# Graph attention layer 1: sums of destination groups alternate between two PSUM places and are copied straight to rows in four pieces

## The reference

```python
def gat_layer(x, W, a_src, a_dst, bias, src, dst, heads, out_c, concat):
    n = x.shape[0]
    h = (x @ W).reshape(n, heads, out_c)
    ...
    ex = jnp.exp(e - m[dst])
    z = jax.ops.segment_sum(ex, dst, num_segments=n)
    alpha = ex / (z[dst] + 1e-16)
    msg = h[src] * alpha[:, :, None]
    out = jax.ops.segment_sum(msg, dst, num_segments=n)
    ...
    return out + bias
...
x = x + _L0_gnn_ref(_layernorm(x, axis=-1), edge_index, ...)
x = x + _L0_ffn_ref(_layernorm(x, axis=-1)[None], ...)[0]
```

## Time and profile before

| | us |
|---|---|
| time, median of 3 runs | 2793.61 |
| lowest and highest of them | 2791.96 to 2797.63 |
| the profiled execution's own time | 2813.5 |
| its span, first to last instruction | 2811.7 |

### The profile page before, as it was taken

One profiled execution on the slowest core, in us unless ns is written; L12 is line 12 of the kernel. 1 busy time (PEld: TensorE's weight loads), 2 busy tenths in 40 slices (PEclk: granted clock), 3 DMA queues, 4 the chain that ended last, 5 costly groups with the idle time before them and its releaser, 6 DMA issues. The chain is left out here.

```text
span 2811.7 us, 45815 instructions
## 1 busy us (share of the span) xinstructions
PE 1794.2 (64%) x14517; PEld 1177.2 (42%) x14518; DVE 1248.1 (44%) x2621; ACT 806.2 (29%) x2172; POOL 1264.5 (45%) x1248
## 2 busy tenths in 40 slices
PE   2747668755555556555678935555555568899970
PEld 1324445433333333333344513333333356677750
DVE  7625658465656556566475051111111126221216
ACT  2400001323333333343122413333333332233320
POOL 4065561076767667710411256666666600112116
PEclk9968889956667566778899966676666777899995
DMA  5313221287877778851797988989898972445549
GB/s 184 97 41 74 68 48 35 95 256 248 253 247 250 254 250 254 261 190 45 189 251 195 259 251 303 316 308 309 306 314 312 315 259 103 129 163 163 165 175 403
DMA packets 185256, 586.03 MB, mean 208 GB/s; under 512 B 40189, under 2 KB 56572, under 8 KB 184930
## 3 DMA queue, kind: packets, MB, share of 16 engines
q0 software_dynamic: 87216, 374.99, 43.4%
q1 hardware_dynamic: 72626, 140.92, 14.9%
q10 hardware_dynamic: 25344, 69.32, 6.4%
HBM read 482.25 MB, written 96.45 MB: 206 GB/s over the span
## 5 line engine op out<-in xcount | busy, mean ns | idle before, releaser
L1437 PE MATMUL acc<-ring,work 128*32 128x192 f32 x1952 | 183.6, 489 | 149.1 <-ACT work L1495 73.3
L1373 POOL DMA_INDIRECT ring<-feat_tab,islot x196 | 231.7, 1182 | 95.7 <-issue 45.7
L1631 PE MATMUL acc<-ring,work 128*32 128x192 f32 (+1 forms) x1952 | 172.7, 494 | 124.6 <-issue 90.7
L862 PE MATMUL acc<-wg,work 128*128 128x384 f32 x600 | 232.1, 532 | 24.2 <-issue 17.4
L1553 POOL DMA_INDIRECT ring<-feat_tab,src_t x196 | 195.3, 996 | 111.9 <-issue 51.8
L1179 PE MATMUL acc<-wg,work 128*128 128x384 f32 x600 | 215.6, 509 | 24.0 <-ACT work L1236 21.5
L812 POOL DMA_INDIRECT edges<-score_tab,src_p x168 | 165.0, 982 | 127.7 <-PE tps L850 56.2
L1410 DVE TENSOR_TENSOR ring<-ring,edges 128x768 f32<-128x768 f32 x196 | 183.0, 956 | 81.7 <-DMA ring<-feat_tab,islot 72.5
L1441 PEld LDWEIGHTS acc<-edges,work 128*32 128x32 f32 x982 | 151.2, 155 | 110.8 <-issue 11.8
L1631 PEld LDWEIGHTS acc<-ring,work 128*32 128x32 f32 x1952 | 90.9, 148 | 184.6 <-issue 168.5
L1631 PE MATMUL acc<-work 128*32 128x192 f32 x1104 | 98.4, 470 | 98.1 <-issue 68.9
(11 more groups left out here) (378 smaller groups left out, 3743.5 us busy)
## 6 DMA issues: line engine op xcount, KB each, us to landing
slot_out<-ring SPq DMA_DIRECT2D x57, 384.0 KB
feat_tab<-work ACTq DMA_DIRECT2D x50, 384.0 KB
ring<-lo_rows SPq DMA_DIRECT2D x49, 256.0 KB
edges<-in_w_slow SPq DMA_DIRECT2D x28, 384.0 KB, 9.9
edges<-in_w_hebb POOLq DMA_DIRECT2D x28, 384.0 KB, 7.7
edges<-in_w_fast POOLq DMA_DIRECT2D x28, 384.0 KB, 9.4
unit_sum<-edges SPq DMA_DIRECT2D x28, 384.0 KB, 6.7
agg_raw<-work ACTq DMA_DIRECT2D x25, 388.0 KB
```

Source lines behind the costliest of these rows:

```text
L862: m = nc.tensor.matmul(acc[:, sl * 2 + c, 0:C // 2], xT[sl][:, k, :], wg[:, k, c * (C // 2):(c + 1) * (C // 2)], start=(k == 0), stop=(k = ...
L1373: pool.indirect_dma_start(rows[k][:, 0:C], None, feat_tab[l], bass.IndirectOffsetOnAxis(ap=islot[:, h * UN + k:h * UN + k + 1], axis=0)).t ...
L1437: m = nc.tensor.matmul(sums_ps[c * WIN:(c + 1) * WIN, 0:CHUNK], hot, row[:, c * CHUNK:(c + 1) * CHUNK], start=start, stop=True, skip_group ...
L1631: m = nc.tensor.matmul(sums_ps[c * WIN:(c + 1) * WIN, 0:n], hot, row[:, c * CHUNK:c * CHUNK + n], start=start, stop=True, skip_group_check ...
```

## The change

The sums of group q now go to PSUM place q % 2 (`acc[:, 0]` or `acc[:, 1]`) and no longer all to `acc[:, 0]`. ACT copies them from there straight to the rows, in four pieces (three of 32 x 192 and one of 32 x 200), with no stage between, and raises `flushed` after the fourth; `flushed` begins at one, so that opening group b waits for the flush of group b-2 instead of b-1. There are two opening matrices, and each is made one group sooner (groups 1 and 2 ahead of the loop, q + 3 after the flush of q), in place of q + 2. The small matmul of `close` writes to another PSUM tensor (`tps`). DVE waits for `flushed` instead of `blk_ready`. The wait for `raw_used`, which was ahead of the copies from stage, is now ahead of the copies out of PSUM. Since the place is part of a matmul's address, PE keeps its number in a register and has each `sums` twice in the code, behind a branch on it.

```diff
@@
-            sums_ps = acc[:, 0, 0:CHUNK + ZC]
-            zp = 3 * WIN
+            next_x = [onehot_x, stage[0][:, 0:WIN]]
@@
-                        dve.wait_ge(blk_ready, (b + 1) * WPB)
+                        dve.wait_ge(flushed, (b + 1) * WPB + 1)
@@
-                            m = nc.tensor.matmul(sums_ps[c * WIN:(c + 1) * WIN, 0:n], hot, row[:, c * CHUNK:c * CHUNK + n],
+                            m = nc.tensor.matmul(acc[c * WIN:(c + 1) * WIN, bank, 0:n], hot, row[:, c * CHUNK:c * CHUNK + n],
@@
-                        nc.tensor.matmul(acc[0:WIN, 1, 0:1], iota_f[:, 0:WIN], iota_f[:, 0:1], start=True, stop=True,
+                        nc.tensor.matmul(tps[0:WIN, 0, 0:1], iota_f[:, 0:WIN], iota_f[:, 0:1], start=True, stop=True,
@@
+                    bank_reg = pe.alloc_register("bank1")
+                    pe.reg_mov(bank_reg, 0)
+
+                    def added(i, k, bank):
+                        if k % BATCH == 0:
+                            pe.wait_ge(hot_in[k // BATCH], i * 16 + 16)
+                        pe.wait_ge(row_in[k], i * 16 + 16)
+                        sums(onehot[:, k, :], k, bank, False).then_inc(tile_mm, 1)
+
+                    def opened(b, k, bank):
+                        pe.wait_ge(open_ready, b)
+                        pe.wait_ge(flushed, b)
+                        sums(next_x[bank], k, bank, True).then_inc(open_mm, 1)
@@
-                            if k % BATCH == 0:
-                                pe.wait_ge(hot_in[k // BATCH], i * 16 + 16)
-                            pe.wait_ge(row_in[k], i * 16 + 16)
-                            sums(onehot[:, k, :], k, t, False).then_inc(tile_mm, 1)
+                            bank = pe.snap(bank_reg, min_val=0, max_val=1)
+                            with pe.If(bank > 0):
+                                added(i, k, 1)
+                            with pe.Else():
+                                added(i, k, 0)
@@
                                 with pe.Fori(b0 + 1, b1 + 1) as b:
-                                    pe.wait_ge(open_ready, b)
-                                    pe.wait_ge(flushed, b)
-                                    sums(onehot_x, k, t, True).then_inc(open_mm, 1)
+                                    pe.reg_mov(bank_reg, b & 1)
+                                    bank = pe.snap(bank_reg, min_val=0, max_val=1)
+                                    with pe.If(bank > 0):
+                                        opened(b, k, 1)
+                                    with pe.Else():
+                                        opened(b, k, 0)
@@
                         if q < NW:
-                            act.wait_ge(open_mm, q)
-                            nc.scalar.activation(onehot_x, hot_open[:, q * WIN:(q + 1) * WIN], ACT.Copy).then_inc(open_ready, 1)
+                            if q >= 3:
+                                act.wait_ge(open_mm, q - 1)
+                            nc.scalar.activation(next_x[q % 2], hot_open[:, q * WIN:(q + 1) * WIN], ACT.Copy).then_inc(open_ready, 1)
@@
+                    act.sem_inc(flushed, 1)
                     act.wait_ge(table_ready, 1)
                     next_hot(1)
+                    next_hot(2)
@@
                             act.wait_ge(closed, q + 1)
-                            nc.scalar.activation(stage[w % 2], sums_ps, ACT.Copy).then_inc(flushed, 1)
-                            next_hot(q + 2)
                             if w == 0 and b >= 2:
                                 act.wait_ge(raw_used, b - 1)
-                            act.wait_ge(flushed, q + 1)
                             for c in range(4):
-                                nc.scalar.activation(raw[b % 2][w * WIN:(w + 1) * WIN, c * CHUNK:(c + 1) * CHUNK],
-                                                     stage[w % 2][c * WIN:(c + 1) * WIN, 0:CHUNK], ACT.Copy)
-                            nc.scalar.activation(raw[b % 2][w * WIN:(w + 1) * WIN, C:ROW],
-                                                 stage[w % 2][zp:zp + WIN, CHUNK:CHUNK + ZC], ACT.Copy).then_inc(blk_ready, 1)
+                                n = CHUNK + ZC if c == 3 else CHUNK
+                                ins = nc.scalar.activation(raw[b % 2][w * WIN:(w + 1) * WIN, c * CHUNK:c * CHUNK + n],
+                                                           acc[c * WIN:(c + 1) * WIN, q % 2, 0:n], ACT.Copy)
+                            ins.then_inc(flushed, 1)
+                            next_hot(q + 3)
```

More of the change, by code:

```diff
@@ L1521, in aggregate_rows @@
                 sem(n + L) for n in ("hot_made", "open_hot", "tile_mm", "open_mm", "ones", "open_table"))
-            closed, flushed, blk_ready, zero_set, batch_mm, raw_used = (
-                sem(n + L) for n in ("closed", "flushed", "blk_ready", "zero_set", "batch_mm", "raw_used"))
+            closed, flushed, zero_set, batch_mm, raw_used = (
+                sem(n + L) for n in ("closed", "flushed", "zero_set", "batch_mm", "raw_used"))
             chain_v, bias_in, sq_in, sq_out, sum_ready, norm_ready = (
@@ L1625, in _, with sums @@
                 def _(pe):
-                    def sums(hot, k, t, start):
+                    def sums(hot, k, bank, start):
                         row = rows[k]
@@ L1642, in _ @@
                     for c in range(4):
-                        m = nc.tensor.matmul(sums_ps[c * WIN:(c + 1) * WIN, :], zeros[:, 0:WIN], zeros, start=True, stop=True,
+                        m = nc.tensor.matmul(acc[c * WIN:(c + 1) * WIN, 0, 0:CHUNK + ZC], zeros[:, 0:WIN], zeros, start=True, stop=True,
                                              skip_group_check=True)
```

## The result

The changed kernel takes 2803.99 us (median of 20 runs, 2796.01 to 2813.37), the kernel before beside it 2796.27 us (20 runs, 2791.38 to 2806.65): a ratio of 1.0024 [1.0013, 1.0034]. The forecast was 2758 us.

What follows compares the result with a forecast made beforehand. The bound was taken as the cycle of PE's drain, late completion and ACT's copy, 6.15 us a group. Falling to 5.74 us over 94.5 cycles gains 39 us, less 3 us for late completions: 2758 us, range 2700 to 2812.

Steps and rivals of the forecast that it cites:

- The drain leaves PE's path: At each group's opening in the gather loop: it waits for flush b-2, so none of PE's 1.87 us idleness is left in principle.
- The sequencer is next: PE's sequencer would pace the gather loop at 5.74 us a group (5.3 to 6.1), 0.79 us a tile.
- POOL has 114 us of slack: In 374 gathers, 1.554 us apart against 1.25 us back to back, POOL stands still 114 us while another engine sets the pace.
- The pace stays: Rival: POOL goes on making four gathers and resting 1.4 us, whatever PE does; about 2790 us; chance 0.14.
- Slower by branches: Rival: additions on PE's sequencer exceed what the drain gave back; 87 us more, 2881 us; chance 0.16.
- Code fetched again: Rival: PE's loop code no longer stays loaded; fetches cost 140 to 390 us, 2900 us and more; chance 0.05.

## Why the prediction was wrong

Two steps of the prediction failed, and each alone takes the gain away: the sequencer's term in the sum was too small, and the time that it was to set free was not free on that kind of chip.

- **The drain leaves PE's path: right.** No opening waits for it any more, hardly one even with 1.6 us added to it (1.4 us in all). But its price was read as 1.87 us of idleness in each group. It is only the part beyond the sequencer's own work between close and opening: with the branches in, about 70 us for the whole part on a late chip and nothing on a prompt one. Without branches, taking the drain away as well gave 605.9 us against 609.3.
- **The sequencer is next: right; its size: wrong.** Predicted 5.74 us a group, measured 6.1, the upper end that I had given. A tile takes 0.84 to 0.97 us, mean about 0.90, against 0.79. The jump costs 0.169 us plus its gap, and there was one register instruction more a tile than the step had: it had one, and the rows show the copy of the register (29 ns) and the value for the wait (37 ns), each with its gap. Taking both away gave 0.16 us a tile. With 0.1 us more a tile the sum is 5.74 + 0.4 = 6.1 us, and the gain is gone: (6.15 - 6.1) x 94.5 = 5 us. That term alone turns 2777 into 2811 us for a profiled run; it had 2801.
- **"POOL has 114 us of slack": wrong on the result's chip.** POOL was waiting, but not for something that a quicker PE brings sooner. With a sequencer of 5.5 us a group, or with no branches at all, the time beside that of the kernel before was 0.9994 and 0.9968. So even a right sum for the sequencer would not have made 2758 us. What POOL waits for there stays open. The prediction also took 19.5 us of its waits for others' than PE's; in the loop POOL waits for PE's tiles alone.
- **"The pace stays"** (0.14, about 2790 us) is where the number came out, and the signs that I named for it are there (gathers in fours, 1.36 us between). Its mechanism isn't shown: the changed kernel's sequencer was busy throughout, and the rests appear on the prompt chip too, where it sets the pace. That two bounds coincide at 603 to 610 us is luck, and it hid the branches' cost.
- **Slower by branches**: I had named the point, 0.50 us added a tile. Measured was 0.51 (0.90 less 0.39), so this case too is what came, at its mildest. Its 2881 us did not come on the result's chip, since the kernel before was as slow there; on a prompt chip it shows in full, 1.0448, a cost of 104 us in the part.
- **Code fetched again: wrong.** The instruction queue of PE's program brought 5 packets at the start of the part (3 before) and none from 1668 us to the end of the loop; 30 in the whole run, 27 before.
- **The clock** fell from 0.67 to 0.57 over the part, where PE's matmuls now stood apart, with the sequencer's gaps between; whether that is the reason no run shows. It cost nothing that can be seen, since the sequencer's pauses add up to 4 us; the prediction did not look at it.
- **The 7 us** by which the median is worse are not found in the two traces: up to the barrier the changed part is 0.4 us shorter in them, parts with the same code differ by up to 13 us (`aggregate`), and the traced run of the kernel before (2813.5 us) is slower than all its 20 others.

The Trainium skill, "Advanced Engine Details and Errata", Control Flow Timing, gives a compare-and-branch at about 108 ns and a jump at about 51 ns. The rows here show 208 ns taken, 65 to 77 ns not taken, and 169 ns for the jump, and the rows decide; with the page's figures the cost comes out too low.

## What to carry to other kernels

A branch per tile on the engine that issues the work costs its duration, a gap, the jump at the end of one side, and whatever the code must compute anew on both sides: here 0.5 us, on top of 0.39 us for the whole tile. Put it in only where the drain that it hides is longer than that, times the tiles of a group, and count first how much of the drain the sequencer's own instructions already hide. And an engine that rests is no proof of slack: before the gain is booked, ask whether it still rests when the engine that it waits for is made quicker. A kernel that leaves out the branches, and with them the right sums, answers that in one run, if it runs on the same kind of chip.

## What the runs showed of the hardware

The kernel before took 2522 to 2531 us on three chips and 2793 to 2814 us on two others and in the result; one of the two gave 2814 us in one batch and 2794 us in the next. The instructions' durations are equal (a gather 0.946 and 0.949 us, the copy out of PSUM 0.337 us); signals are later. Parts that the change doesn't touch differ too, from barrier to barrier: `products_scores_first` takes 415 to 424 us against 341 to 346, `aggregate` 658 to 674 against 583 to 604; `experts` has 335 to 339 us on both. So the chip belongs to the result: the same change costs 104 us in the part on one kind of chip and nothing that can be seen there on the other. A sequencer instruction costs its duration and 0.03 to 0.06 us more: a wait of 0.051 us cost 0.077 us a tile.
